# TensorE's order moved one part ahead in a mixture-of-experts step, with two PSUM banks for each kind of result

## The chip, the cores and the metric

The kernel is one program on one core of a Trainium2 chip. The metric is the device time of one execution in microseconds, shown as the median of several executions; one further execution was recorded by the hardware profiler. TensorE is called PE here, VectorE DVE, ScalarE ACT, GpSimd POOL, and SP is the engine that issues most of the DMAs.

## The reference

Four sequences (batches) of 512 tokens and 512 features. Each goes first through a selective state-space block that works on a context input, and then through a mixture of experts. Cut to what matters:

```python
# front: the state-space block, per batch
u = silu(conv(in_proj(ctx)))                     # 512 channels x 512 tokens
delta = softplus(dt_proj(x_proj(u)))             # B, C (16 rows each) from x_proj too
for t in tokens:                                 # 16 states per channel
    state = state * exp(delta_t * A) + (delta_t * u_t) * B_t
    y_t = sum(state * C_t, over the 16 states)
x = x + tanh(g_xattn) * (y + D * u) * silu(layernorm(x))
# feed-forward: the shared expert and 7 routed ones, with top-3 weights w_e
n = layernorm(x)
out = (silu(n @ Ws1) * (n @ Wsg)) @ Ws2
for e in range(7):
    out += w_e * ((silu(n @ W1[e]) * (n @ Wg[e])) @ W2[e])
x = x + tanh(g_ffn) * out
```

All weight matrices of the experts are 512 x 512, and every expert is computed on all tokens.

## The kernel before

The feed-forward work is cut into 32 steps: 4 batches times 8 experts (the shared one is expert 0). Each 512 x 512 x 512 product is made from operands split into a high and a low half, in three passes. In a step, TensorE makes four "up" parts (`up(step, j)`, bank `ps_h1[j % 2]`) and four "gate" parts (`gate(step, j)`, the single bank `ps_hg`), 12 matmuls each, alternately, and then the four outputs (`down_high` and `down_low`, banks `ps_y[i % 3]`), also 12 matmuls each: tiles 0 and 1 together, then tile 2, then tile 3. A step has 144 such matmuls.

Between the parts the other engines make the hidden tile j: ACT's tanh of the up part into `h_tmp[j % 2]` (L857, `t_done`), DVE's first product (L1219, `m_done`), DVE's product with the gate part (L1224, `h_made`), ACT's high half (L863, `hh_ready`), and POOL's low half (L1363, `hl_ready`). DVE adds each output tile to `acc` (`add_out`, L1214, `acc_done`).

The state-space block of the next batch is woven into the steps of the present one, by hand, in slots: `between(0)` to `between(11)` on TensorE and on DVE, two for each hidden tile and four in the outputs. The steps of experts 2 to 6 (five in each of the first three batches; "state steps" below) carry most of it. For each of the 16 states, slots give DVE two multiplications (`bmul`, L1089) and two scans (`scan`, L1098) over 1024 columns each, and four sums (`sum_rows`, L1104); TensorE four groups of four transposes (`state_to_rows`, L538); ACT four decays (`decay`, L791). The first transposes of a state wait for its second scan: on TensorE these stand in the slots 0, 4 and 8 of a state step, and the scan that slot 8 waits for is in DVE's slot 7. ACT runs three decays after each high half, in order; each decay waits for the scan that last read its buffer. In the step of expert 7, DVE finishes the block: `make_y` (L1127), `residual` (L1135, L1138), mean and variance, `make_x2` (L1143), and two of the next convolution's taps (L1000). Then TensorE transposes x2 (L547), ACT and DVE split it (L823, L1151), and the next batch's shared step begins.

In batch 0 the weights are split into halves as they come (ACT: `split_hi`, L848; POOL: L1358, L1369, L1375) and stored; SP loads the stored halves in the later batches (`fetch_part`), each part after TensorE has read its forerunner. SP works through one hand-written queue. The last batch has no state-space work beside it.

Of the kernel before, what the change touches and what calls it, by code (L numbers as in the profile page):

```python
# [28 lines left out]
def gated_block(nc, t, out):  # L29
# [20 lines left out]
    with ExitStack() as ctx:  # L50
# [77 lines left out]
        conv_ps = [ps_h1[0], ps_h1[1], ps_hg, ps_y[0]]  # L128
# [328 lines left out]
        def _(pe):  # L457
# [12 lines left out]
            def in_proj(m, et):  # L470
# [3 lines left out]
                else:  # L474
                    bank = ps_y[1 + et % 2]
# [101 lines left out]
            def up(step, j):  # L577

                weights_ready(0, step, j)
                if j >= 2:  # L580
# [17 lines left out]
            def down_high(step, tiles):  # L598

                for j in range(T):  # L600
                    pe.wait_ge(hh_ready, T * step + j + 1)
                    weights_ready(2, step, j)
                    for i in tiles:
                        three_passes(ps_y[i % 3][:], [h_hi[:, j, i * P:(i + 1) * P]], [half(2, j, 0), half(2, j, 1)],
                                     ((0, 0), (0, 1)), j == 0, False)

            def down_low(step, tiles):

                for i in tiles:
                    for j in range(T):  # L610
                        pe.wait_ge(hl_ready, T * step + j + 1)
                        mm = pe.matmul(ps_y[i % 3][:], h_lo[:, j, i * P:(i + 1) * P], half(2, j, 0),  # L612
                                       start=False, stop=j == T - 1)
                    mm.then_inc(y_done, 1)

            def step_(step, between=lambda g: None, before_down=None):
# [6 lines left out]
                if some(step):  # L623
                    pe.wait_ge(acc_done, T * step)
# [836 lines left out]
```

## Time and profile before

| | |
|---|---|
| median of 3 executions | 1498.68 us (1497.59 to 1501.57) |
| profiled execution, its own time | 1496.58 us |
| profiled execution, span from first to last instruction | 1494.5 us |
| TensorE busy | 1397.6 us (94%) |
| DVE busy | 1053.1 us (70%) |
| ACT busy | 510.0 us (34%) |
| POOL busy | 453.6 us (30%) |
| mean granted TensorE clock | 0.968 |

The busy time of TensorE is modelled from pipelined matmuls, so how far apart matmuls start says more than how long one is shown. The granted clock is a share of 2.4 GHz.

### The profile page before, as it was taken

To read this page: it belongs to the slowest core of one execution; us is meant where nothing else is said; L and a number is where in the kernel's file an instruction comes from. 1 tells how busy PE (TensorE), PEld (TensorE's weight loads), DVE (VectorE), ACT (ScalarE), POOL (GpSimd) and SP (SyncE) were. 2 spreads that over 40 slices of the span, in tenths; PEclk is the share of its full clock that TensorE was granted. 3 is DMA by queue.
4 is the path that set the end of the run, shared out by engine and by line. 5 is a ranking of instruction groups with operands and counts; after the bars stand their busy time and mean duration, and the time that the engine had idled before them with its cause. 6 is when DMAs were issued, how large, how long until landed. Compare 5 with 4: busy or idle time off the path is not lost.

```text
span 1494.5 us, 18163 instructions
## 1 busy us (share of the span) xinstructions
PE 1397.6 (94%) x6311; PEld 1078.6 (72%) x6311; DVE 1053.1 (70%) x1259; ACT 510.0 (34%) x855; POOL 453.6 (30%) x240
## 2 busy tenths in 40 slices
PE   8599869999999989999999979999999999999999
PEld 4244456877777776787787867787778878888887
DVE  5898855899998974588999874689999853222222
ACT  3676625544444323432322223432332211111111
POOL 3200004687777721123323211122332211111111
PEclk9599989999999999999999999999999999999999
DMA  6111634567765574455555564455555554655552
GB/s 206 43 64 57 252 121 171 204 248 272 243 244 206 212 249 141 143 192 179 177 173 181 174 247 128 143 184 179 185 176 172 184 191 156 210 194 191 189 168 84
DMA packets 90796, 266.36 MB, mean 178 GB/s; under 512 B 11472, under 2 KB 11600, under 8 KB 90336
## 3 DMA queue, kind: packets, MB, share of 16 engines
q1 hardware_dynamic: 85472, 258.39, 51.0%
q10 hardware_dynamic: 5248, 6.96, 1.3%
q8 instruction: 47, 0.77, 0.2%
q14 instruction: 29, 0.24, 0.0%
HBM read 207.39 MB, written 57.93 MB: 178 GB/s over the span
## 4 chain that ended last, share of the span: by engine, by line
PE 68%; DVE 18%; issue 6%; ACT 5%; DMA 2%; SPq 1%; POOL 0%; ACTq 0%; DVEq 0%; POOLq 0%
PE ps_hg L461 19%; PE ps_h L461 18%; PE ps_y L461 12%; PE ps_y L612 7%; DVE st L1098 7%; PE ps_mid L538 5%; DVE y_rows L1104 3%; ACT dA L791 2%; PE ps_h L530 2%; DVE st L1089 1%; DVE u L1000 1%; PE ps_mid L508 1%; DVE h_tmp L1224 1%; PE ps_mid L501 1%; DVE h_tmp L1219 1%
## 5 line engine op out<-in xcount | busy, mean ns | idle before, releaser
L1363 POOL TENSOR_TENSOR h_lo<-h_tmp,h_hi 128x512 fp32r<-128x512 f32 x128 | 280.8, 2194 | 781.7 <-ACT h_hi L863 781.7
L461 PE MATMUL ps_h<-x_hi,w_split 128*128 128x512 f32 x1024 | 350.8, 404 | 9.0 <-issue 4.6
L461 PE MATMUL ps_hg<-x_hi,wg_split 128*128 128x512 f32 x1024 | 349.8, 403 | 3.4 <-DVE h_tmp L1224 3.4
L1098 DVE TENSOR_TENSOR_SCAN st<-dA,st 128x1024 f32<-128x1024 f32 x128 | 298.5, 2341 | 0.0
L461 PE MATMUL ps_y<-w_split,h_hi 128*128 128x512 f32 x1024 | 258.2, 400 | 0.8 <-ACT h_hi L863 0.8
L461 PEld LDWEIGHTS ps_h<-x_hi,w_split 128*128 128x128 f32 x1024 | 195.1, 191 | 50.8 <-issue 6.9
L863 ACT ACTIVATE h_hi<-h_tmp 128x512 fp32r<-128x512 f32 x128 | 81.0, 632 | 430.6 <-DVE h_tmp L1224 430.6
L461 PEld LDWEIGHTS ps_hg<-x_hi,wg_split 128*128 128x128 f32 x1024 | 195.3, 191 | 44.4 <-issue 4.2
L461 PEld LDWEIGHTS ps_y<-w_split,h_hi 128*128 128x128 f32 x1024 | 190.3, 190 | 40.0 <-ACT h_hi L863 2.0
L1219 DVE SCALAR_TENSOR_TENSOR h_tmp<-h_tmp,ps_h 128x512 f32<-128x512 f32 x128 | 87.8, 686 | 182.8 <-ACT h_tmp L857 182.4
L461 PE MATMUL ps_hg<-x_lo,wg_split 128*128 128x512 f32 x512 | 202.1, 395 | 0.0
L461 PE MATMUL ps_h<-x_lo,w_split 128*128 128x512 f32 x512 | 201.7, 394 | 0.0
L538 PEld LDWEIGHTS ps_mid<-ident,st 128*128 128x128 f32 x1024 | 124.1, 141 | 94.3 <-issue 49.7
L1089 DVE TENSOR_TENSOR st<-u,b_all 128x1024 f32<-128x1024 f32 x128 | 179.2, 1411 | 10.4 <-PE ps_mid L538 10.3
L538 PE MATMUL ps_mid<-ident,st 128*128 128x128 f32 x1024 | 154.8, 277 | 29.7 <-DVE st L1098 27.1
L791 ACT ACTIVATE dA<-delta,neg_A 128x511 f32<-128x511 f32 x256 | 168.3, 710 | 34.5 <-DVE st L1098 27.9
L857 ACT ACTIVATE h_tmp<-ps_h 128x512 f32<-128x512 f32 x128 | 76.0, 593 | 298.8 <-PE ps_h L461 298.6
L1224 DVE TENSOR_TENSOR h_tmp<-h_tmp,ps_hg 128x512 f32<-128x512 f32 x128 | 87.6, 685 | 101.7 <-PE ps_hg L461 101.4
L1104 DVE SCALAR_TENSOR_TENSOR y_rows<-ps_mid,c_cols,y_rows 128x512 f32<-128x512 f32 x192 | 142.0, 740 | 0.0
L612 PE MATMUL ps_y<-w_split,h_lo 128*128 128x512 f32 x512 | 134.4, 394 | 0.0
L1214 DVE SCALAR_TENSOR_TENSOR acc<-ps_y,coef,acc 128x512 f32<-128x512 f32 x112 | 82.5, 736 | 59.1 <-PE ps_y L612 58.9
L461 PEld LDWEIGHTS ps_h<-x_lo,w_split 128*128 128x128 f32 x512 | 98.3, 192 | 18.5
(140 smaller groups left out, 1133.5 us busy)
## 6 DMA issues: line engine op xcount, KB each, us to landing
w_split<-split_scratch SPq DMA_DIRECT2D x192, 512.0 KB, 4.9
wg_split<-split_scratch SPq DMA_DIRECT2D x96, 512.0 KB, 4.2
split_scratch<-w_split SPq DMA_DIRECT2D x64, 512.0 KB, 4.3
b_all<-xd_scratch SPq DMA_DIRECT2D x64, 256.0 KB, 4.0
split_scratch<-wg_split SPq DMA_DIRECT2D x32, 512.0 KB, 3.1
w_raw<-in_W_dram SPq DMA_DIRECT2D x14, 1024.0 KB, 7.6
wg_raw<-in_Wg_dram SPq DMA_DIRECT2D x7, 1024.0 KB, 10.0
dA<-in_x_dram SPq DMA_DIRECT2D x4, 1024.0 KB, 11.0
```

The source lines that it names most:

```text
L461: mm = pe.matmul(out_, lhs[a], rhs[c], start=first and q == 0, stop=last and q == len(sides) - 1)
L538: mm = pe.transpose(ps_mid[bank][:, et * P:(et + 1) * P], st[n % 2][:, et, i * P:(i + 1) * P], ident[:])
L612: mm = pe.matmul(ps_y[i % 3][:], h_lo[:, j, i * P:(i + 1) * P], half(2, j, 0), start=False, stop=j == T - 1)
L791: act.activation(dA[odd][:, et, 1:L], delta[:, et, 1:L], ACT.Exp, scale=neg_A[:, et, n:n + 1]).then_inc(da_ready, 1)
L863: act.activation(h_hi[:, j, :], h_tmp[j % 2][:], ACT.Copy).then_inc(hh_ready, 1)
L1089: dve.tensor_tensor(st[odd][:, two], u[:, two], b_all[odd][:].rearrange("p (a l) -> p a l", a=1).broadcast_to([P, 2, L]), ALU.mult).then_i ...
L1098: dve.tensor_tensor_scan(flat[1], flat[0], flat[1], 0.0, ALU.mult, ALU.add).then_inc(scan_done, 1)
L1104: dve.scalar_tensor_tensor(out=y_rows[:, i, :], in0=ps_mid[bank][:], scalar=c_cols[:, i, n:n + 1], in1=y_rows[:, i, :], op0=ALU.mult, op1= ...
L1214: dve.scalar_tensor_tensor(out=acc[:, i, :], in0=ps_y[i % 3][:], scalar=scale, in1=before[:, i, :], op0=ALU.mult, op1=ALU.add).then_inc(ac ...
L1219: dve.scalar_tensor_tensor(out=h_tmp[j % 2][:], in0=h_tmp[j % 2][:], scalar=1.0, in1=ps_h1[j % 2][:], op0=ALU.add, op1=ALU.mult).then_inc( ...
L1224: dve.tensor_tensor(h_tmp[j % 2][:], h_tmp[j % 2][:], ps_hg[:], ALU.mult).then_inc(h_made, 1)
L1363: pool.tensor_tensor(h_lo[:, j, :], h_tmp[j % 2][:], h_hi[:, j, :].bitcast(F32), ALU.subtract).then_inc(hl_ready, 1)
```

## The change

TensorE's order in a step becomes: up and gate parts 1 to 3 of this expert, then up and gate part 0 of the *next* expert, then this expert's four outputs, one after the other. The other engines' orders follow: the tanh and the two products of tile 0 of the next step come before this step's `add_out`s; its high half waits for `y_done`, since `h_hi` is single. The slots 0 to 11 keep their numbers, and now lie around parts 1, 2, 3, 0' and the outputs 0 to 3. The last step of each batch (expert 7) has no part ahead; the shared step begins with its own part 0. The eight PSUM banks are divided anew: `ps_hg` gets two, `ps_y` two instead of three. SP's queue is not changed.

```diff
-        ps_hg = ctx.enter_context(nc.psum_tensor("ps_hg", [P, L], F32))
-        ps_y = [ctx.enter_context(nc.psum_tensor(f"ps_y{i}", [P, L], F32)) for i in range(3)]
+        ps_hg = [ctx.enter_context(nc.psum_tensor(f"ps_hg{i}", [P, L], F32)) for i in range(2)]
+        ps_y = [ctx.enter_context(nc.psum_tensor(f"ps_y{i}", [P, L], F32)) for i in range(2)]
@@ tensor
             def gate(step, j):
                 weights_ready(1, step, j)
-                if j >= 1:
-                    pe.wait_ge(h_made, T * step + j)
-                product(ps_hg, 1, j).then_inc(hg_done, 1)
+                if some(T * step + j - 1):
+                    pe.wait_ge(h_made, T * step + j - 1)
+                product(ps_hg[j % 2], 1, j).then_inc(hg_done, 1)
-            def down_high(step, tiles):
-            def down_low(step, tiles):
+            def down(step, i):
+                if some(T * step + i - 1):
+                    pe.wait_ge(acc_done, T * step + i - 1)
+                for j in range(T):
+                    pe.wait_ge(hh_ready, T * step + j + 1)
+                    weights_ready(2, step, j)
+                    three_passes(ps_y[i % 2][:], [h_hi[:, j, i * P:(i + 1) * P]], [half(2, j, 0), half(2, j, 1)],
+                                 ((0, 0), (0, 1)), j == 0, False)
                 for j in range(T):
+                    pe.wait_ge(hl_ready, T * step + j + 1)
+                    mm = pe.matmul(ps_y[i % 2][:], h_lo[:, j, i * P:(i + 1) * P], half(2, j, 0),
+                                   start=False, stop=j == T - 1)
+                mm.then_inc(y_done, 1)
+            def step_(step, ahead=True, between=lambda g: None):
+                for j in range(1, T):
                     up(step, j)
-                    between(2 * j)
+                    between(2 * j - 2)
                     gate(step, j)
-                    between(2 * j + 1)
+                    between(2 * j - 1)
-                down_high(step, (0, 1))
-                between(2 * T)
-                down_low(step, (0, 1))
-                between(2 * T + 1)
-                down_high(step, (2,))
-                down_low(step, (2,))
-                between(2 * T + 2)
-                pe.wait_ge(acc_done, T * step + 1)
-                down_high(step, (3,))
-                down_low(step, (3,))
-                between(2 * T + 3)
+                if ahead:
+                    up(step + 1, 0)
+                between(2 * T - 2)
+                if ahead:
+                    gate(step + 1, 0)
+                between(2 * T - 1)
+                for i in range(T):
+                    down(step, i)
+                    between(2 * T + i)
@@ scalar
+            def h_high(step, j):
+                act.wait_ge(h_made, T * step + j + 1)
+                if j == 0 and some(step):
+                    act.wait_ge(y_done, T * step)
+            def step_(step, ahead=True, between=lambda j: None, after=lambda j: None):
+                for j in range(1, T):
+                    tanh(step, j)
+                    if first_round(step + 1):
+                        split_hi(step + 1, 0, w1h, j)
+                    between(j)
+                    h_high(step, j)
+                    if first_round(step + 1):
+                        split_hi(step + 1, 1, wgh, j)
+                    after(j)
+                if ahead:
+                    tanh(step + 1, 0)
+                between(T)
+                if ahead:
+                    h_high(step + 1, 0)
+                if first_round(step + 1):
+                    split_down(step + 1)
+                if first_round(step + 2):
+                    split_front(step + 2)
@@ vector
+                for j in range(1, T):
+                    hidden(step, j, lambda: between(2 * j - 2))
+                    between(2 * j - 1)
+                if ahead:
+                    hidden(step + 1, 0, lambda: between(2 * T - 2))
+                else:
+                    between(2 * T - 2)
+                between(2 * T - 1)
+                for i in range(T):
+                    between(2 * T + i)
+                    add_out(i)
@@ gpsimd
+                for j in range(1, T):
+                    if first_round(step + 1):
+                        split_up(step + 1, j)
+                    h_low(step, j)
+                    if first_round(step + 1):
+                        split_gate(step + 1, j)
+                    between(j)
+                if ahead:
+                    h_low(step + 1, 0)
+                if first_round(step + 1):
+                    split_down(step + 1)
+                if first_round(step + 2):
+                    split_front(step + 2)
```

`split_front(step)` splits tile 0 of an expert's up and gate weights. In the shared step, the router's columns move from behind gate 0 to behind up 1, and on DVE the convolution's taps stand in tile 0's two products while `front_silu` moves behind tile 1's first product.

## Rows read from the trace of the kernel before

**Rows 1.** The page: busy time by engine, and the chain that ended last.
```profile
PE 1397.6 (94%) x6311; PEld 1078.6 (72%) x6311; DVE 1053.1 (70%) x1259; ACT 510.0 (34%) x855; POOL 453.6 (30%) x240
...
PE 68%; DVE 18%; issue 6%; ACT 5%; DMA 2%; SPq 1%; POOL 0%; ACTq 0%; DVEq 0%; POOLq 0%
```

**Rows 2.** Waits of PE in the whole span: releaser, us in total, times, longest us.
```profile
PE ps_mid L538 <- DVE st L1098: 27.1, 28, 4.2
PE ps_mid L547 <- DVE x_lo L1151: 12.5, 4, 5.1
...
PE ps_hg L461 <- DVE h_tmp L1224: 3.4, 2, 2.8
```

**Rows 3.** Windows: state steps of batches 0 and 1, and a step of batch 3.
```profile
430.00:475.00 45.00, 41.31 (x196) 32.78 (x195) 40.62 (x38) 18.91 (x34) 33.49 (x16) 0.96 0.64 229
690.00:730.00 40.00, 39.09 (x195) 31.48 (x194) 36.24 (x37) 12.27 (x20) 12.80 (x4) 1.00 0.54 177
...
1328.00:1361.00 33.00, 33.00 (x147) 27.35 (x146) 8.77 (x13) 4.92 (x8) 5.15 (x4) 1.00 0.57 191
```

**Rows 4.** Chain in a step of batch 3, one of its up parts: start us, us, what.
```profile
1295.31 2.72 PE ps_h L461 x12
```

**Rows 5.** PE timeline, outputs of a state step in batch 1, with idle before.
```profile
715.79 0.39 PE L461 MATMUL ps_hg<-x_hi,wg_split 128*128 128x512 f32 x1
...
716.62 3.91 PE L461 MATMUL ps_y<-w_split,h_hi 128*128 128x512 f32 x16
720.80 0.66 PE L538 MATMUL ps_mid<-ident,st 128*128 128x128 f32 x4 [0.28 <-DVE st L1098]
...
729.92 0.48 PE L461 MATMUL ps_h<-x_hi,w_split 128*128 128x512 f32 x1
```

**Rows 6.** DVE and ACT timelines, the same stretch.
```profile
716.01 1.21 DVE L1089 TENSOR_TENSOR st<-u,b_all 128x1024 f32<-128x1024 f32 x1
717.14 0.68 DVE L1224 TENSOR_TENSOR h_tmp<-h_tmp,ps_hg 128x512 f32<-128x512 f32 x1
...
718.40 2.28 DVE L1098 TENSOR_TENSOR_SCAN st<-dA,st 128x1024 f32<-128x1024 f32 x1
...
722.77 0.74 DVE L1214 SCALAR_TENSOR_TENSOR acc<-ps_y,coef,acc 128x512 f32<-128x512 f32 x1
...
713.50 0.72 ACT L791 ACTIVATE dA<-delta,neg_A 128x511 f32<-128x511 f32 x1 [1.06 <-DVE st L1098]
714.13 0.58 ACT L857 ACTIVATE h_tmp<-ps_h 128x512 f32<-128x512 f32 x1
```

**Rows 7.** Timelines of a state step in batch 0: PE, then ACT, then DVE.
```profile
448.50 0.66 PE L538 MATMUL ps_mid<-ident,st 128*128 128x128 f32 x4 [2.15 <-DVE st L1098]
...
465.35 0.66 PE L538 MATMUL ps_mid<-ident,st 128*128 128x128 f32 x4 [1.00 <-DVE st L1098]
...
429.72 2.19 ACT L848 ACTIVATE w_split<-w_raw 128x512 fp32r<-128x512 f32 x4 [7.65 <-PE ps_y L612]
432.94 0.60 ACT L857 ACTIVATE h_tmp<-ps_h 128x512 f32<-128x512 f32 x1 [1.02 <-PE ps_h L461]
...
434.83 2.19 DVE L1089 TENSOR_TENSOR st<-u,b_all 128x1024 f32<-128x1024 f32 x1
```

**Rows 8.** Timelines at the end of batch 0: DVE, then PE.
```profile
539.78 0.69 DVE L1219 SCALAR_TENSOR_TENSOR h_tmp<-h_tmp,ps_h 128x512 f32<-128x512 f32 x1 [0.84 <-ACT h_tmp L857]
...
546.43 0.75 DVE L1214 SCALAR_TENSOR_TENSOR acc<-ps_y,coef,acc 128x512 f32<-128x512 f32 x1
...
556.03 0.74 DVE L1214 SCALAR_TENSOR_TENSOR acc<-ps_y,coef,acc 128x512 f32<-128x512 f32 x1
...
558.71 1.94 PE L547 MATMUL ps_mid<-ident,st 128*128 128x128 f32 x8 [5.10 <-DVE x_lo L1151]
```

**Rows 9.** PE timelines of the shared steps of batches 0 and 1.
```profile
222.62 0.47 PE L461 MATMUL ps_hg<-x_hi,wg_split 128*128 128x512 f32 x1 [2.83 <-DVE h_tmp L1224]
...
598.49 5.54 PE L461 MATMUL ps_y<-w_split,h_hi 128*128 128x512 f32 x16
```

More of the change, by code:

```diff
@@ L648, in shared_step @@
                 pe.wait_ge(*taken(b, column_place(b, T - 1)))
-                step_(STEPS * b, between)
+                up(STEPS * b, 0)
+                gate(STEPS * b, 0)
+                step_(STEPS * b, True, between)
             def state_sums(m, first):
@@ L901, in after, with ahead_1, after_1 @@
                         front_ccols(m)
[L902 to L919 removed]
+                tanh(STEPS * b, 0)
+                h_high(STEPS * b, 0)
+                if first_round(STEPS * b + 1):
+                    split_front(STEPS * b + 1)
+                if m is not None:
+                    front_tanh(m)
+                router_columns(b)
+                step_(STEPS * b, True, between, after)
+            def batch(b, m):
+                def ahead_1(j):
+                    if j == T:
+                        decays(m, T, 2 * T)
+                def after_1(j):
+                    if j == 1:
                         router_exp(b)
                         front_z(m, (0, 1))
[L922 removed]
+                    if j == 2:
                         decays(m, 0, 2)
[L924 removed]
+                    if j == 3:
                         front_z(m, (2, 3))
                         decays(m, 2, T)
[L927 to L928 removed]
                 if some(b):
@@ L1203, in router, with hidden, step_ @@
                 assert done[0] == links
-            def step_(step, e, between=lambda p: None):
+            def hidden(step, j, between=None):
+                dve.wait_ge(t_done, T * step + j + 1)
+                dve.scalar_tensor_tensor(out=h_tmp[j % 2][:], in0=h_tmp[j % 2][:], scalar=1.0, in1=ps_h1[j % 2][:],
+                                         op0=ALU.add, op1=ALU.mult).then_inc(m_done, 1)
+                if between:
+                    between()
+                dve.wait_ge(m_done, T * step + j + 1)
+                dve.wait_ge(hg_done, T * step + j + 1)
+                dve.tensor_tensor(h_tmp[j % 2][:], h_tmp[j % 2][:], ps_hg[j % 2][:], ALU.mult).then_inc(h_made, 1)
+            def step_(step, e, ahead=True, between=lambda p: None):
                 def add_out(i):
@@ L1331, in last @@
                         front_conv(m + 1, (1,))
-                step_(STEPS * b, None, shared)
-                step_(STEPS * b + 1, 0, first_routed)
+                hidden(STEPS * b, 0, lambda: front_conv(m, range(DC - 1) if b == 0 else (DC - 2,)))
+                step_(STEPS * b, None, True, shared)
+                step_(STEPS * b + 1, 0, True, first_routed)
                 for e in range(2, NE):
-                    step_(STEPS * b + e, e - 1, lambda p: slot(m, 3 * (e - 2) + 1 + p // T, p % T))
-                step_(STEPS * b + NE, NE - 1, last)
+                    step_(STEPS * b + e, e - 1, True, lambda p: slot(m, 3 * (e - 2) + 1 + p // T, p % T))
+                step_(STEPS * b + NE, NE - 1, False, last)
             for b in range(NB - 1):
@@ L1424, in _ @@
             power(x2var, x2rstd, 0)
-            batch(0, 1)
-            with pool.Fori(1, NB - 1) as b:
+            for b in range(NB - 1):
                 batch(b, b + 1)
-            with pool.Fori(0, STEPS) as e:
+            shared_step(NB - 1)
+            with pool.Fori(1, NE) as e:
                 step_(STEPS * (NB - 1) + e)
+            step_(STEPS * NB - 1, False)
 def kernel(**inputs):
```

165 lines of the change are left out of this document (59 added, 106 removed).

## The prediction

> **What bounds the kernel now.** I read the page first, then PE's waits, then windows by stage, then the chain and the timelines of one step of each kind. The page has PE busy for 94% of the span and on 68% of the chain; DVE has most of the rest [rows 1]. A step of batch 3 is pure TensorE: 33.00 us busy in 33, its clock whole [rows 3], and twelve matmuls take 2.72 us, so one starts every 0.227 us [rows 4]. All 144 need 32.6 us, and nothing waits. So batch 3's seven routed steps have nothing to win, whatever the order. The two waits that the new banks address are small: the gate bank's 3.4 us, in 2 places; waits for scans are 27.1 us, in 28 [rows 2].
>
> In the state steps DVE is nearly as full as PE: 36.24 us of 40 in batch 1, 40.62 of 45 in batch 0 [rows 3]. There the end is set by turns: by PE, and in slots 4 and 8 by the scan that the transposes wait for. At the batch boundaries DVE's chain alone sets it, with PE idle for 5.10 us [rows 8].
>
> **State steps of batches 1 and 2.** The last gate part's last matmul starts at 715.79, the outputs at 716.62. Before slot 8 stand 16 output matmuls, 16 x 0.227 = 3.63 us, so TensorE is free for the transposes at 720.25; it starts them at 720.80 [rows 5]. What comes last is DVE: second product 717.14, sum, scan 718.40 + 2.28 = 720.68 [rows 6]. In the new order only output 0 stands there, 12 matmuls, 2.72 us: TensorE is free 0.91 us earlier. The scan isn't: DVE's slots keep their places around the fourth hidden tile, and that tile's tanh is late because ACT stands at a decay that waits 1.06 us for a scan (713.50, then the tanh at 714.13) [rows 6]; three decays still stand ahead of the tanh. So the wait grows by 0.91 us, and the four matmuls that covered it are done later: 10 steps x 0.9 = +9. The bound below is 0 (the scan comes earlier by as much), above 1.2 each.
>
> The two output banks cost nothing there: output 2 needs `add_out(0)`, which starts at 722.77 and takes 0.74 [rows 6], while TensorE is in output 1 until about 720.80 + 0.4 + 2.9 = 724.1. Output 3 needs `add_out(1)`, after one more sum and scan (0.7 + 2.2), about 727; TensorE comes there 2.9 + 0.4 us after 724.4, about 727.7. It is close.
>
> **State steps of batch 0.** The same 0.9 us. Besides, ACT is released when the outputs are done (429.72), splits four tiles in 2.19 and does the tanh at 432.94, for which it has waited 1.02 us [rows 7]. Now it makes the high half of tile 0 (about 0.6), four splits, 2.19, and two more for the expert after next, 2 x 0.55 = 1.1: 3.9 us instead of 3.2, so the tanh is 0.7 late, and DVE with it. DVE has no slack behind: TensorE stands 2.15 us at 448.50 and 1.00 at 465.35 for its scans [rows 7]. That makes 1.6. POOL's work also comes in one longer run (low half of tile 0, four splits, two more), under DVE's multiplications, of which one takes 2.19 us in batch 0 and 1.21 in batch 1 [rows 6, 7]; one more stretched would add 1.0. I take 2.0, between 1.6 and 2.6: 5 steps, +10 (8 to 13). The Trainium skill (GPSIMD Engine Reference, 1 Specifications) says that GpSimd shares its SBUF interfaces with VectorE and contends with VectorE instructions that have two SBUF inputs, which these have; the rows agree. By that rule the upper end, 13, would be the sum's term; by the rows it may be either.
>
> **Batch boundaries.** TensorE has done up and gate 0 of the last expert ahead, 2 x 2.72 = 5.44 us, inside the step before. The last step is shorter by that, but DVE's chain (sums, make_y, residual, statistics, x2, taps) starts at the same slot as before and so 5.44 us later in TensorE's work. TensorE had idle time there, which it can't use for work already done. DVE gains back one tile's wait, 0.84, and its two products, about 1.2 [rows 8]: 2.1. Net +3.3, at two boundaries. `add_out(0)` at 546.43 stands behind residual and statistics [rows 8]; with two banks output 2 waits for it, about 3 us, and output 3 for the next behind x2. Where the taps follow (they end before the last `add_out`, 556.03) DVE hides this. At the third boundary no taps follow: there I take 4.2, between 3.3 and the whole 5.4. Sum +10.8 (5 to 16). If DVE's chain did not end last, it would be 0.
>
> **What it gains.** In batch 0's shared step gate 1 waits 2.83 us for the single bank, behind the convolution's taps [rows 9]; now nothing waits, but `front_silu` moves back on DVE, behind a tanh that stands behind the router's columns, and `xproj` needs it. I keep 2, between 0 and 2.83 and the slower clock after it. In the shared steps of batches 1 and 2 the first 16 output matmuls take 5.54 us [rows 9] against 3.91 [rows 5], waiting for ACT's high half, for which two parts now stand as cover: 2 x 1.6 = 3.2. Together -5 (-3 to -9). In batch 3's last step the high half of tile 3 is needed 6 matmuls, 1.4 us, after the gate part instead of 12: +0.5. SP's queue is as before: the ahead part's weights wait for `h1_done` counts that now come earlier; I cost it at 0, since the fetch follows the output weights by a few descriptors, issued at the end of the previous step, and TensorE needs it some 16 us later (6 x 2.72). If SP stood at a `load_b` there, the whole delay would show.
>
> **Sum.** 9 + 10 + 10.8 - 5 + 0.5 = +25.3 against the profiled execution, 1496.58 us (span 1494.5 and 2.1 around it): 1521.9. The median is 2.1 above that execution: 1524.0 us.
>
> **Rivals.** Noise is about 0.3%, 4.5 us, from 1498.7.
> - *Forecast, 0.62:* slot 8's wait deeper, batch 0 later, boundaries later: 1524, its own range 1511 to 1534.
> - *The clock falls too, 0.15.* Batch 0's windows show a granted clock of 0.96 where TensorE stood for 2.15 us, batch 1's 1.00 with short waits [rows 3, 5, 7]. The new waits at slot 8 are 1.2 us in batches 1 and 2 and near 2 in batch 0. If they suffice, each step loses 0.04 x 45 = 1.8 us: 10 to 15 steps, +18 to +27, about 1547. Against it: 1.2 us is nearer to the 0.28 to 1.0 us after which nothing is seen than to 2.15. The Trainium skill (TensorE: Matmul & The Clock Gate, Part 1) says that the half rate is the default and activity releases it; it would speak for this case.
> - *Faster, 0.08.* The part ahead gives DVE's scan its time, because the decay that holds the fourth tanh becomes free sooner. It decides if the scan ends 1.4 us sooner relative to the gate part: then the 27.1 us of scan waits go [rows 2], and with the -5 and the boundaries' +10.8 the time is 1498.7 - 27 - 5 + 11 = 1478. For it: ACT has no splits in the fourth tile any more. Against: batch 1 has no splits at all and waits the same way. The Trainium skill (Perfetto Trace Analysis, Optimization Strategy) reads one gap that repeats as a sign of too few buffers, as PSUM; the repeating gap here waits for a scan, not for a bank, which the trace says against it.
> - *Only the boundaries cost, 0.15.* DVE's slots move up by the 0.9 us, and POOL's run hides: 10.8 - 5 + 0.5, 1505; with the boundaries' lower bound 1499. That the order does nothing falls here, half of it within the noise.
>
> **Numbers.** Slower 0.83 (the first two and half of the last), same 0.09, faster 0.08. The range reaches to the last rival's upper half and to the clock's: 1502 to 1543.
>
> **What would show it.** In the new profile: the wait of `ps_mid` L538's transposes for scans grows from 27 to about 45 us; state steps of batches 1 and 2 0.9 us longer than the 40 us that a window holds now, those of batch 0 2 us longer than 45 [rows 3]; PE's idle before x2's transposes moves partly to outputs 2 and 3; batch 3's steps stay at 32.6; the 2.83 and the 5.54 go. I am wrong if slot 8's wait stays at 0.3 us, if the granted clock in batches 1 and 2 falls under 1.00, or if TensorE waits for a DMA ahead of a part 0.

## The result, and the profile after

The changed kernel takes 1523.18 us (median of 4, 1522.20 to 1527.27) against 1498.13 (4 runs, 1495.32 to 1501.57) of the kernel before on the same chip: ratio 1.0171, 95% interval 1.0143 to 1.0200. The profiled execution takes 1523.53, its span 1521.7. The prediction said 1524.0, slower.

The page of the changed kernel (busy time, chain), for [rows 1]:

```profile
PE 1401.4 (92%) x6311; PEld 1077.9 (71%) x6311; DVE 1048.1 (69%) x1259; ACT 507.7 (33%) x855; POOL 418.4 (27%) x240
...
PE 63%; DVE 20%; issue 7%; ACT 6%; DMA 2%; SPq 1%; ACTq 0%; POOL 0%; DVEq 0%
```

The busy times are nearly the same but for POOL's (418.4 for 453.6); PE's share of the chain fell from 68% to 63%. Its waits, for [rows 2] (us in total, times, longest):

```profile
PE ps_mid L538 <- DVE st L1117: 42.9, 31, 4.2
...
PE ps_mid L547 <- DVE x_lo L1170: 11.2, 4, 4.6
...
PE ps_y L609 <- POOL h_lo L1387: 4.7, 3, 1.6
...
PE ps_y L461 <- DVE acc L1243: 3.1, 3, 2.1
```

The gate bank's 3.4 us are gone, and the waits for scans grew from 27.1 to 42.9 (about 45 was forecast). The windows, for [rows 3]: two of batch 0, one of batch 1, one of batch 3. After the stretch and its length stand the busy us (and instructions) of PE, PE's weight loads, DVE, ACT and POOL, then the granted clock, the share of the DMA engines and GB/s.

```profile
352.00:397.00 45.00, 40.24 (x184) 31.96 (x184) 38.43 (x36) 16.76 (x30) 28.37 (x16) 0.92 0.62 226
420.00:465.00 45.00, 40.23 (x197) 32.19 (x196) 39.53 (x37) 18.27 (x32) 28.59 (x17) 1.00 0.62 220
700.00:740.00 40.00, 38.19 (x190) 30.69 (x189) 34.92 (x37) 11.54 (x19) 11.16 (x4) 1.00 0.50 178
1290.00:1323.00 33.00, 33.00 (x148) 27.31 (x147) 13.77 (x38) 5.04 (x9) 5.15 (x4) 1.00 0.54 191
```

PE has 38.19 us of 40 in batch 1, where it had 39.09, at a whole clock. The outputs of such a step, PE, then DVE, then ACT, for [rows 5, 6]:

```profile
734.47 0.39 PE L461 MATMUL ps_hg<-x_hi,wg_split 128*128 128x512 f32 x1
...
735.30 2.10 PE L461 MATMUL ps_y<-w_split,h_hi 128*128 128x512 f32 x8
737.24 1.08 PE L609 MATMUL ps_y<-w_split,h_lo 128*128 128x512 f32 x4
739.49 0.65 PE L538 MATMUL ps_mid<-ident,st 128*128 128x128 f32 x4 [1.17 <-DVE st L1117]
...
735.82 0.68 DVE L1232 TENSOR_TENSOR h_tmp<-h_tmp,ps_hg 128x512 f32<-128x512 f32 x1
...
737.08 2.28 DVE L1117 TENSOR_TENSOR_SCAN st<-dA,st 128x1024 f32<-128x1024 f32 x1
...
732.18 0.72 ACT L787 ACTIVATE dA<-delta,neg_A 128x511 f32<-128x511 f32 x1 [1.06 <-DVE st L1117]
732.81 0.58 ACT L851 ACTIVATE h_tmp<-ps_h 128x512 f32<-128x512 f32 x1
```

Set the last gate matmul to zero in both kernels: the tanh starts at -1.66, the scan at +2.61, in both. ACT's decay waits for a scan for 1.06 us in both. DVE and ACT did not move against TensorE; only four matmuls of cover went, and the wait is 1.17 instead of 0.28.

The whole span by stretches, from the starts of the same matmuls in both traces: from a batch's first matmul to the end of expert 1's outputs, the five state steps, and the last expert with the boundary. 5.44 us are put back where a part ran ahead, so that each column holds the same work.

| us | start | shared + expert 1: batch 0, 1, 2 | state steps | last + boundary | batch 3 |
|---|---|---|---|---|---|
| before | 207.0 | 92.8, 87.8, 87.8 | 217.9, 199.3, 199.4 | 44.4, 47.4, 40.3 | 270.3 |
| changed | 208.2 | 91.3, 87.6, 87.0 | 227.5, 203.8, 203.8 | 47.8, 51.4, 44.1 | 269.4 |
| difference | +1.1 | -1.6, -0.2, -0.8 | +9.6, +4.5, +4.4 | +3.4, +4.0, +3.8 | -0.9 |

The differences add to the 27.2 us by which the spans differ.

### The profile page after: what moved, and what is told of

The parts are those of the page before. It is cut to its first block, busy times and chain, and to the rows that moved or that the text cites. A ratio compares the mean times of both kernels' runs of the same rounds, so it can differ in the third digit from the quotient of the medians.

```text
span 1521.7 us, 18382 instructions
## 1 busy us (share of the span) xinstructions
PE 1401.4 (92%) x6311; PEld 1077.9 (71%) x6311; DVE 1048.1 (69%) x1259; ACT 507.7 (33%) x855; POOL 418.4 (27%) x240
## 4 chain that ended last, share of the span: by engine, by line
PE 63%; DVE 20%; issue 7%; ACT 6%; DMA 2%; SPq 1%; ACTq 0%; POOL 0%; DVEq 0%
PE ps_hg L461 18%; PE ps_h L461 16%; PE ps_y L461 12%; DVE st L1117 8%; PE ps_y L609 6%; PE ps_mid L538 5%; DVE y_rows L1123 3%; ACT dA L787 2%; PE ps_h L530 2%; DVE h_tmp L1232 1%; DVE h_tmp L1226 1%; ACT w_split L844 1%; DVE u L1019 1%; PE ps_mid L508 1%; DVE st L1108 1%
## 5 line engine op out<-in xcount | busy, mean ns | idle before, releaser
L1387 POOL TENSOR_TENSOR h_lo<-h_tmp,h_hi 128x512 fp32r<-128x512 f32 x128 | 252.7, 1974 | 893.2 <-ACT h_hi L858 893.2
L1117 DVE TENSOR_TENSOR_SCAN st<-dA,st 128x1024 f32<-128x1024 f32 x128 | 304.9, 2392 | 0.0
L461 PE MATMUL ps_y<-w_split,h_hi 128*128 128x512 f32 x1024 | 264.1, 399 | 5.0 <-DVE acc L1243 3.1
L1226 DVE SCALAR_TENSOR_TENSOR h_tmp<-h_tmp,ps_h 128x512 f32<-128x512 f32 x128 | 87.6, 684 | 229.3 <-ACT h_tmp L851 228.9
L461 PEld LDWEIGHTS ps_y<-w_split,h_hi 128*128 128x128 f32 x1024 | 187.6, 189 | 45.4 <-DVE acc L1243 5.4
L538 PE MATMUL ps_mid<-ident,st 128*128 128x128 f32 x1024 | 156.5, 279 | 46.5 <-DVE st L1117 42.9
L1108 DVE TENSOR_TENSOR st<-u,b_all 128x1024 f32<-128x1024 f32 x128 | 169.9, 1338 | 10.7 <-PE ps_mid L538 10.5
L609 PE MATMUL ps_y<-w_split,h_lo 128*128 128x512 f32 x512 | 138.8, 392 | 4.7 <-POOL h_lo L1387 4.7
L609 PEld LDWEIGHTS ps_y<-w_split,h_lo 128*128 128x128 f32 x512 | 96.2, 188 | 27.3 <-POOL h_lo L1387 6.4
```

Of the source, the lines that this page charges most:

```text
L461: mm = pe.matmul(out_, lhs[a], rhs[c], start=first and q == 0, stop=last and q == len(sides) - 1)
L538: mm = pe.transpose(ps_mid[bank][:, et * P:(et + 1) * P], st[n % 2][:, et, i * P:(i + 1) * P], ident[:])
L609: mm = pe.matmul(ps_y[i % 2][:], h_lo[:, j, i * P:(i + 1) * P], half(2, j, 0), start=False, stop=j == T - 1)
L1108: dve.tensor_tensor(st[odd][:, two], u[:, two], b_all[odd][:].rearrange("p (a l) -> p a l", a=1).broadcast_to([P, 2, L]), ALU.mult).then_i ...
L1117: dve.tensor_tensor_scan(flat[1], flat[0], flat[1], 0.0, ALU.mult, ALU.add).then_inc(scan_done, 1)
L1226: dve.scalar_tensor_tensor(out=h_tmp[j % 2][:], in0=h_tmp[j % 2][:], scalar=1.0, in1=ps_h1[j % 2][:], op0=ALU.add, op1=ALU.mult).then_inc( ...
```

## The experiments

Each was run with the kernel before beside it on the same chip; ratios are to that, medians are in the text. "State steps" are those of the table. The start phase, in which all kernels do the same work, takes 204.1 to 208.3 us in the profiled executions, without an order by kernel that I can see, so I read the stretches and not the spans.

### What the order costs, in parts

Three kernels fill the square between before and the changed one: the new banks with outputs 0 and 1 in pairs or all one by one, each with and without the part ahead.

**outs_alone.** Before's order of parts, the new banks, outputs one by one:

```diff
+                product(ps_hg[j % 2], 1, j).then_inc(hg_done, 1)
...
-                down_high(step, (0, 1))
-                between(2 * T)
-                down_low(step, (0, 1))
-                between(2 * T + 1)
...
+                for i in range(T):
+                    down(step, i)
+                    between(2 * T + i)
```

> The order of parts before the change, with the changed kernel's banks (two for the gate, two for the outputs) and its outputs one after the other; no part ahead. Theory (slot 8 loses cover because one output, 12 matmuls, stands ahead of it instead of 16): state steps of batches 1 and 2 take 0.9 us more than the 40.0 of the kernel before, batch 0's about 0.9 more, the boundaries stay as before, the 2.8 us wait for the gate bank goes: about +9 +4.5 -3 = +10, 1509 us. Rival (the part ahead itself makes the state steps longer): state steps stay at 40.0, 1495 to 1498 us.

Measured: 1548.42 us, ratio 1.0342 (1.0325 to 1.0359), slower than either theory had it. State steps 226.2, 214.8, 214.8. Its waits, and a step's outputs:

```profile
PE ps_y L609 <- POOL h_lo L1350: 28.2, 18, 1.9
PE ps_mid L538 <- DVE st L1085: 16.4, 16, 4.2
PE ps_y L461 <- ACT h_hi L850: 13.4, 26, 2.2
```

```profile
732.52 0.73 PE L461 MATMUL ps_y<-w_split,h_hi 128*128 128x512 f32 x2 [0.28 <-ACT h_hi L850]
735.78 0.50 PE L609 MATMUL ps_y<-w_split,h_lo 128*128 128x512 f32 x1 [1.83 <-POOL h_lo L1350]
```

Output 0 alone needs the fourth high half after 6 matmuls and the fourth low half after 11; in pairs they are needed after 12 and 19. Both come late, so TensorE stands ahead of slot 8 and the scan is no longer what it waits for. What I had seen as a loss at slot 8 alone is a loss of cover, and the next thing to be late takes it.

**banks.** The same without the outputs' order: before with only the banks dealt anew.

```diff
-        ps_hg = ctx.enter_context(nc.psum_tensor("ps_hg", [P, L], F32))
-        ps_y = [ctx.enter_context(nc.psum_tensor(f"ps_y{i}", [P, L], F32)) for i in range(3)]
+        ps_hg = [ctx.enter_context(nc.psum_tensor(f"ps_hg{i}", [P, L], F32)) for i in range(2)]
+        ps_y = [ctx.enter_context(nc.psum_tensor(f"ps_y{i}", [P, L], F32)) for i in range(2)]
...
+                for i in (2, 3):
+                    pe.wait_ge(acc_done, T * step + i - 1)
```

> Before's order with only the banks dealt anew: two for gate and two for the outputs, so that output 2 shares its bank with output 0 and output 3 with output 1; outputs 0 and 1 are still done in pairs, and no part runs ahead. Theory (banks cost nothing, the order does it): state steps of batches 1 and 2 stay at 40.0 us, those of batch 0 at 42.4 to 44.6, the 3.4 us of waits for the gate bank go, the boundaries lose at most 1 us each by output 2 waiting for add_out(0): 1494 to 1501 us. Rival (the third output bank was worth something in every step): output 2 waits for add_out(0) in the state steps, which then take 41 us or more: 1510 us and up.

Measured: 1504.36 us, ratio 1.0051 (1.0034 to 1.0067), between the theories. A state step of batch 1 takes 40.39 instead of 40.04 us, and a routed step of batch 3 33.01 instead of 32.64. In batch 3 output 2 starts 0.2 us late, behind `add_out(0)`; in batch 1 it is output 3 that starts 0.3 us late, behind `add_out(1)`. The third output bank was worth about 0.35 us a step. The second gate bank bought nothing: its waits go, but in batch 0's shared step TensorE then waits 3.8 us for ACT's `xdbl`, and that stretch of the table is 94.2 us for 92.8.

**pairs.** The changed kernel with before's order of the outputs:

```diff
-                for i in range(T):
-                    down(step, i)
-                    between(2 * T + i)
+                high(step, (0, 1))
+                between(2 * T)
+                low(step, (0, 1))
+                between(2 * T + 1)
+                for i in (2, 3):
+                    pe.wait_ge(acc_done, T * step + i - 1)
+                    high(step, (i,))
+                    low(step, (i,))
+                    between(2 * T + i)
```

> The changed kernel, part ahead and banks as they are, but outputs 0 and 1 in pairs as before: 16 high matmuls of both, slot 8, the 8 low ones, slot 9. Theory of the prediction (the step order costs by the four matmuls that no longer stand between the fourth gate part and slot 8): the wait at slot 8 falls from 1.5 back to 0.6 us, state steps of batches 1 and 2 go from 40.9 to 40.0 us, those of batch 0 lose about as much; boundaries stay as in the changed kernel (about 4 us each above before): 1523 - 14 = 1509 us, between 1506 and 1514. Rival (it is the part ahead that makes DVE late, whatever the outputs' order): steps stay at 40.9 and the time at 1520 to 1525 us.

Measured: 1518.16 us, ratio 1.0145 (1.0129 to 1.0162). The steps of batches 1 and 2 do what the theory says: 40.07 us for 40.96, state steps 199.5 for 203.8, and batch 0's lose 3.6. The waits for scans are back at 29.6:

```profile
PE ps_mid L538 <- DVE st L1132: 29.6, 29, 4.2
...
PE ps_y L461 <- DVE acc L1258: 9.0, 4, 2.3
```

The total misses the expected 1506 to 1514. Pairs with two banks wait for `add_out(0)`: 2.3 us at each of the three boundaries (the fourth place, 2.1 us, is in batch 0 and in the changed kernel too), and a step of batch 3 takes 0.37 us more. Against the changed kernel the state steps lose 12.2 us, but the boundaries (47.2, 52.0 and 45.4 now) put back 1.3, batch 3 2.0 and the shared stretches 3.1.

The square, as ratios to before: pairs 1.0051 without and 1.0145 with the part ahead; one by one 1.0342 without and 1.0171 with it. So neither the part ahead nor the outputs' order has a price of its own. The part ahead costs 0.9% beside pairs and gains 1.7% where the outputs go one by one, whose late halves it covers.

### Where the transposes stand

**late8.** The changed kernel with TensorE's slot 8 behind output 1, beside slot 9. DVE's order is as it was.

```diff
-                for i in range(T):
-                    down(step, i)
-                    between(2 * T + i)
+                down(step, 0)
+                down(step, 1)
+                between(2 * T)
+                between(2 * T + 1)
+                for i in range(2, T):
+                    down(step, i)
+                    between(2 * T + i)
```

> The changed kernel with TensorE's slots 8 and 9 both behind output 1; no other engine's order changes. Theory (the wait at slot 8 is bare idle that another output can cover, 1.3 us in 15 state steps): the wait of the transposes for scans falls by some 18 us, state steps of batches 1 and 2 from 40.95 to 39.7 to 40.0, and the time by 14 to 19 us, to about 1507. Rival (DVE's chain bounds the state step and TensorE's wait only moves to output 2 or 3 or to slot 4): within 4 us of 1523.

Measured: 1513.52 us, ratio 1.0121 (1.0100 to 1.0142). State steps 224.6, 199.4, 199.4: batches 1 and 2 are at before's 199.3, and the 0.9 us a step are shown to be the missing cover ahead of slot 8. The time fell by 9.7 us where 14 to 19 were expected: the state steps give back 11.7, but batch 3 has a slow stretch at its start in this execution (272.0 us for 269.4) that the changed kernel's has not.

**late48.** late8, and in the state steps slot 4 behind gate 3:

```diff
                     up(step, j)
-                    between(2 * j - 2)
+                    if j < T - 1 or not late:
+                        between(2 * j - 2)
                     gate(step, j)
+                    if j == T - 1 and late:
+                        between(2 * j - 2)
                     between(2 * j - 1)
```

> The changed kernel with TensorE's slot 8 behind output 1 together with slot 9 (as in late8) and, in the state steps, slot 4 behind the gate part 3 instead of the up part 3. Theory (the waits for scans at slots 4 and 8 are a matter of where TensorE's order places the transposes, and DVE has the slack): the 0.96 us at slot 4 go as the 1.5 us at slot 8 did: state steps of batches 1 and 2 fall from 40.0 in late8 to 39.3 us, batch 0's by 1 to 2: 1500 to 1507 us. Rival (DVE's chain sets the steps once slot 8 is late): the steps stay at 40.0, the wait moves to slot 5 or to the up part of the step ahead: 1512 to 1516 us.

Measured: 1498.38 us (10 runs), ratio 1.0013 (1.0002 to 1.0025), a little below the theory's range. State steps 222.0, 194.5, 194.5: two moved places give back nearly all that the change lost. **before_late** does the same to the kernel before (slot 4 behind gate 2's products, slot 8 behind the low passes of outputs 0 and 1):

```diff
                     up(step, j)
-                    between(2 * j)
+                    if j != 2 or not late:
+                        between(2 * j)
                     gate(step, j)
+                    if j == 2 and late:
+                        between(2 * j)
...
                 down_high(step, (0, 1))
-                between(2 * T)
                 down_low(step, (0, 1))
+                between(2 * T)
                 between(2 * T + 1)
```

> The kernel before, its banks and its order, with slot 4 behind the gate part and slot 8 behind the low passes of outputs 0 and 1 in the state steps. Theory (the scan waits are placement only): its 27 us of waits for scans fall under 8, the state steps of batches 1 and 2 go from 40.0 to 39.0 us, batch 0's by 1 to 2 each: 1478 to 1488 us. Rival (without a part ahead the order has no more cover: output 0's low pass and the next step's first tile wait instead): 1493 to 1503 us.

Measured: 1485.03 us, ratio 0.9922 (0.9905 to 0.9938), faster than before. Its PE waits:

```profile
PE ps_y L612 <- POOL h_lo L1369: 11.4, 13, 1.4
PE ps_mid L538 <- DVE y_rows L1110: 10.4, 13, 1.5
...
PE ps_mid L538 <- DVE st L1104: 4.2, 1, 4.2
```

Of the 27.1 us for scans [rows 2] 4.2 are left, at one place outside the state steps. State steps 213.2, 196.0, 195.9 (39.35 us a step, 39.0 was expected). With late slots the whole change (part ahead, banks and outputs' order together) is worth 1.5 us in each of batches 1 and 2 (194.5), and costs 8.8 in batch 0 and 3.4, 4.2 and 3.8 at the boundaries.

### Batch 0: the splits

**splitgap.** The changed kernel; ACT and POOL do the tile-0 splits of the expert after next in the fourth tile's gap, ahead of the high half and not in the run behind the outputs:

```diff
+                if first_round(step + 2):
+                    act.wait_ge(h_made, T * (step + 1) + 1)
+                    split_front(step + 2)
                 if ahead:
                     h_high(step + 1, 0)
                 if first_round(step + 1):
                     split_down(step + 1)
-                if first_round(step + 2):
-                    split_front(step + 2)
```

> The changed kernel with tile 0's weights of the expert after next split on ACT and POOL before the high half of tile 0, where both stand idle in the outputs (5 to 9 us on ACT, 15 on POOL), instead of behind the splits of the output weights. Theory (ACT's two more splits make the first tanh of a step late, and POOL's run stretches DVE's multiplications): only batch 0's state steps change, each 1 to 2 us shorter, 1515 to 1518 us. Rival (batch 0's slot 4 waits for DVE's own work, stretched by POOL wherever POOL's splits stand): batch 0 within 2 us in total, about 1522.

Measured: 1517.16 us, ratio 1.0152 (1.0122 to 1.0182). Only batch 0's state steps answer to the edit, 224.9 for 227.5; 4 us of the span lie in the start phase. So 2.6, less than the theory's 5 to 10 and near the rival's 2: slot 4 still waits 2.9 to 3.2 us in four of the five steps. In the second step it waits 2.14, and there the scan that it waits for takes 2.27 us, in the others 3.3 to 3.4.

**late48_split** has this edit on top of late48.

> late48 and splitgap together: slots 4 and 8 late, and ACT and POOL do the two tile-0 weight splits of the expert after next in the fourth tile's gap. Theory (in batch 0 the long run of splits behind the outputs holds the tanh and so DVE): batch 0's state steps fall from 44.5 to 43 us or less, five of them, 1491 to 1494 us. Rival (with the slots late the tanh is no longer what TensorE waits for; POOL's run under DVE's multiplications and scans is): batch 0's state steps stay within 0.5 us of 44.5, 1496 to 1500 us.

Measured: 1488.79 us, ratio 0.9945 (0.9923 to 0.9966), below the theory's range. Batch 0's state steps are 214.8 for 222.0, a step 42.5 to 43.4. The first tanh of a step comes at least 0.5 us earlier in all five steps, but the last step gains nothing by it (43.37 us for 43.23). The first step gains 2.2, its tanh 1.0 us earlier. The three in the middle gain 1.3 to 1.9 us, and in each of them one scan takes 2.28 us that took 3.37. That scan and POOL's work beside it, in late48, then in late48_split:

```profile
371.88 1.28 POOL L1400 TENSOR_TENSOR wg_split<-wg_raw,wg_split 128x512 fp32r<-128x512 f32 x1
371.94 3.37 DVE L1124 TENSOR_TENSOR_SCAN st<-dA,st 128x1024 f32<-128x1024 f32 x1
```

```profile
369.70 2.28 DVE L1125 TENSOR_TENSOR_SCAN st<-dA,st 128x1024 f32<-128x1024 f32 x1
369.86 3.20 POOL L1395 TENSOR_TENSOR h_lo<-h_tmp,h_hi 128x512 fp32r<-128x512 f32 x1 [0.19 <-ACT h_hi L865]
```

So 1.1 us of each middle step goes with where POOL's instructions lie against DVE's scans, and an earlier tanh alone gained nothing in the last one. The edit moves the splits of both engines at once, so no run separates ACT's share from POOL's. One edit alone gave 2.6, since TensorE then stood at slots 4 and 8 all the same.

### The boundaries

**bound.** The changed kernel with the last step's slots two parts earlier, packed two by two:

```diff
                def last(q):
+                    if q < 2:
+                        slot(m, DS, 2 * q)
+                        slot(m, DS, 2 * q + 1)
+                    elif q < 2 * T:
+                        last_(q + 2)
```

> The changed kernel with the last step of each of the first three batches getting its state sums and the end of the block two parts earlier (TensorE's four groups behind up 1 and gate 1, DVE's in the same two slots, everything after them two slots earlier). Theory (the boundary costs 3.4 to 3.9 us each because DVE's chain starts two parts late in TensorE's work): each boundary 3 to 5 us shorter, the waits of output 2 for acc gone, 1509 to 1514 us, about 11 less than the changed kernel. Rival (the boundary is set by the transposes of x2 and ACT's and DVE's split of them, not by when the chain starts): within 3 us of 1523.

Measured: 1529.46 us, ratio 1.0225 (1.0202 to 1.0248), outside both ranges; the boundaries grow to 48.5, 52.5 and 46.7. Packed transposes stop TensorE for 1.7 and 1.2 us, since a pair shares what it waits for on DVE, and `add_out(0)` now stood behind x2:

```profile
555.48 1.92 DVE L1163 TENSOR_SCALAR st<-z,mv,rstd 128x512 f32<-128x512 f32 x4 [1.12 <-POOL rstd L1387]
557.32 1.60 DVE L1244 SCALAR_TENSOR_TENSOR acc<-ps_y,coef,acc 128x512 f32<-128x512 f32 x2
```

This edit brought new waits of its own, so it does not tell the theories apart.

**edge** does: late48 with the last expert's part 0 not run ahead. The last step does four tiles as before, and expert 6's slots 6 and 7 stand behind its output 0.

```diff
-                    step_(STEPS * b + e, True, state_sums(m, 3 * (e - 2)), True)
-                step_(STEPS * b + NE, False, state_sums(m, DS - 1))
+                    step_(STEPS * b + e, e < NE - 1, state_sums(m, 3 * (e - 2)), True)
+                last_step(STEPS * b + NE, state_sums(m, DS - 1))
```

> late48 with the last expert's first up and gate part not run ahead: expert 6's step ends without a part ahead (its slots 6 and 7 stand behind output 0), and the last step of a batch does its four tiles with DVE's slots where they are in the kernel before. Batch 3 keeps its part ahead. Theory of the prediction (the boundaries lose because DVE's closing chain starts one part later in TensorE's work): the last step and boundary fall from late48's 47.8, 51.3 and 44.2 us to about 44.4, 48.2 and 42.1 us, the values of outs_alone, -8 to -9 in all; expert 6's step, without cover for the high and low halves, gets 1.5 to 3 us longer in each of three batches, +4 to +9: 1493 to 1501 us. Rival (the boundaries lose by the outputs' order and the two banks, not by the part ahead): they stay within 1 us of late48's and the time rises to 1502 to 1510 us.

Measured: 1504.97 us, ratio 1.0053 (1.0036 to 1.0070). From the last step's first matmul to the next batch's it takes 43.7, 48.1 and 42.1 us: what the theory says, and 9.2 less than late48's 47.8, 51.3 and 44.2. So the boundaries lose mainly by the part ahead; the outputs' order and banks leave -0.7, +0.7 and +1.8 against before. The time itself lies in the rival's range, because expert 6's step costs more than I had put: +3.4 in batches 1 and 2, +6.7 in batch 0. The place, at the end of batch 1, POOL and then PE:

```profile
840.12 3.17 POOL L1416 TENSOR_TENSOR h_lo<-h_tmp,h_hi 128x512 fp32r<-128x512 f32 x1 [2.96 <-ACT h_hi L878]
...
843.35 0.50 PE L609 MATMUL ps_y<-w_split,h_lo 128*128 128x512 f32 x1 [1.60 <-POOL h_lo L1416]
...
849.76 2.11 PE L461 MATMUL ps_y<-w_split,h_hi 128*128 128x512 f32 x8 [1.07 <-DVE acc L1267]
```

Taking the part away at one place uncovers what it covered there, by one and a half times what it saved.

### A version faster than both

**third_bank.** before_late (the cut is against it, and the next one's against third_bank; both hold for the state steps), whose third output bank lets output 2's high passes run before the low ones of output 0:

```diff
                 down_high(step, (0, 1))
+                down_high(step, (2,))
-                down_low(step, (0, 1))
+                down_low(step, (0,))
                 between(2 * T)
+                down_low(step, (1,))
                 between(2 * T + 1)
-                down_high(step, (2,))
                 down_low(step, (2,))
```

> before_late (before's order and banks, slots 4 and 8 late), and in the state steps the third output bank is used: the high passes of output 2 stand right behind those of outputs 0 and 1, then low 0, slot 8, low 1, slot 9, low 2. Theory (what is left in a state step is one wait of 0.74 us of output 0's low pass for POOL's low half of tile 3, which eight more matmuls cover): 15 steps, those of batches 1 and 2 fall from 39.35 to 38.6 us: 1485 - 11 = 1474 us. Rival (output 3 then waits for add_out(0), which comes eight matmuls later on DVE): steps stay at 39.3, 1483 to 1487 us.

Measured: 1479.42 us, ratio 0.9882 (0.9865 to 0.9898), between the theories. The wait for POOL is gone, but in batches 1 and 2 a step takes 39.24 us for 39.35: the cover was spent at the next late thing, slot 0.

```profile
682.62 0.65 PE L538 MATMUL ps_mid<-ident,st 128*128 128x128 f32 x4 [0.57 <-DVE st L1108]
```

Batch 0, at 206.7 for 213.2, has most of the gain; the boundaries take 3.1 us more in all. **slots_048** moves slot 0 behind gate 0 as well:

```diff
-                    if j != 2 or not late:
+                    if j in (1, 3) or not late:
                         between(2 * j)
                     gate(step, j)
-                    if j == 2 and late:
+                    if j in (0, 2) and late:
                         between(2 * j)
```

> third_bank with slot 0 behind gate part 0 as well, beside slot 1, in the state steps. In third_bank the one wait left over 0.3 us in a state step of batch 1 is 0.72 us at slot 0, whose scan is released late because output 0's sum is later. Theory (placement again: DVE has slack over the step, 36.5 us of 39.2): the wait goes, steps of batches 1 and 2 fall from 39.24 to 38.5 us: 1479 - 10 = 1469 to 1473 us. Rival (DVE's and ACT's chain of decays, scans and hidden tiles now sets the step's length): steps stay at 39.0 to 39.3, the wait shows at slot 4 or 8 instead: 1476 to 1481 us.

Measured: 1472.94 us, ratio 0.9837 (0.9821 to 0.9854). Steps of 38.4 us; state steps 206.6, 191.8, 191.8. A window of batch 1:

```profile
700.00:740.00 40.00, 40.00 (x203) 33.04 (x202) 37.71 (x37) 12.93 (x22) 14.42 (x5) 1.00 0.56 187
```

TensorE is busy for all of it, with before's PSUM banks and no part ahead.

## Why the prediction was right, point by point

The total was right, and the terms for batches 1 and 2 and the boundaries were right by their mechanism. That batch 0 came out close is in part luck, and only half of the gains came, as said below. (The chances as written add up to 0.845 for slower, not 0.83.)

- **State steps of batches 1 and 2, +9:** measured +4.5 and +4.4, by the mechanism named: 1.17 for 0.28 us of idle at slot 8 in four steps of each batch, and 0.58 for none in the fifth. late8 and pairs each take it away, by either road (transposes later, or 16 matmuls ahead of them).
- **State steps of batch 0, +10:** measured +9.6, but made up otherwise. The 0.9 us at slot 8 did not come in four of the five steps, where it waits 1.1 us for 1.0; only in the last does it wait 1.78 for none. ACT's run and the late tanh did come, after and in the order ACT, POOL, DVE, PE:

```profile
350.49 0.63 ACT L858 ACTIVATE h_hi<-h_tmp 128x512 fp32r<-128x512 f32 x1 [8.64 <-PE ps_y L609]
351.03 2.70 ACT L844 ACTIVATE w_split<-w_raw 128x512 fp32r<-128x512 f32 x5
...
353.63 0.62 ACT L844 ACTIVATE wg_split<-wg_raw 128x512 fp32r<-128x512 f32 x1
354.15 0.57 ACT L851 ACTIVATE h_tmp<-ps_h 128x512 f32<-128x512 f32 x1
...
352.78 6.05 POOL L1399 TENSOR_TENSOR w_split<-w_raw,w_split 128x512 fp32r<-128x512 f32 x4
...
354.76 0.69 DVE L1226 SCALAR_TENSOR_TENSOR h_tmp<-h_tmp,ps_h 128x512 f32<-128x512 f32 x1 [2.40 <-ACT h_tmp L851]
...
370.22 1.11 PE L538 MATMUL ps_mid<-ident,st 128*128 128x128 f32 x4 [3.21 <-DVE st L1117]
```

  From release to tanh ACT needs 3.66 us, 0.44 more than before's 3.22 (0.7 was forecast), DVE stands 2.40 for it, and TensorE's wait at slot 4 is 3.21 for 2.15 [rows 7]. But in the four steps behind the first the late tanh is made up for before slot 4: its scan starts 16.3 us after the step's first matmul before the change and 16.2 after it. What grew there is the scan, by 1.08 us, as much as the wait. (In the first of the five the scan was long before the change too, and it starts later.) DVE and then POOL before the change, and POOL and then DVE after it:

```profile
446.17 2.27 DVE L1098 TENSOR_TENSOR_SCAN st<-dA,st 128x1024 f32<-128x1024 f32 x1
446.33 3.19 POOL L1363 TENSOR_TENSOR h_lo<-h_tmp,h_hi 128x512 fp32r<-128x512 f32 x1 [0.19 <-ACT h_hi L863]
```

```profile
366.75 1.26 POOL L1393 TENSOR_TENSOR wg_split<-wg_raw,wg_split 128x512 fp32r<-128x512 f32 x1
366.82 3.35 DVE L1117 TENSOR_TENSOR_SCAN st<-dA,st 128x1024 f32<-128x1024 f32 x1
```

  After the change POOL is in the middle of its run when the scan starts. So the forecast's POOL term (one more stretched instruction of DVE's, 1.0) is the one that came, in four steps; its 0.9 at slot 8 and ACT's 0.7 mostly did not. By the distances between matmul starts, slot 4 has 5.1 of the 9.6, slot 8 2.1 (1.7 of them in the last step), waits for `y_rows` 1.5 and the slower clock about 1.4; small differences take back 0.5.
- **Boundaries, +10.8:** measured +11.2. outs_alone, without the part ahead, has 44.4, 48.2 and 42.1: so the part ahead is all of the 3.4 at the first boundary, 3.2 of the 4.0 at the second and 2.0 of the 3.8 at the third, and edge shows it too. The rest is the outputs' order and the banks, which the forecast did not count there. The detail was less right as well. Outputs 2 and 3 were to wait for sums, output 2 about 3 us; such waits are 0.48 and 0.51 us at the boundaries (the third and longest, 2.09, is in batch 0's step of expert 1), since TensorE comes to them later by 0.57 and 1.57 us of waits in output 0. PE, then DVE, at the end of batch 0:

```profile
559.63 2.14 PE L461 MATMUL ps_y<-w_split,h_hi 128*128 128x512 f32 x8 [0.48 <-DVE acc L1243]
571.15 1.94 PE L547 MATMUL ps_mid<-ident,st 128*128 128x128 f32 x8 [4.59 <-DVE x_lo L1170]
574.69 0.79 PE L461 MATMUL ps_h<-x_hi,w_split 128*128 128x512 f32 x1 [1.60 <-DVE x_lo L1170]
...
558.83 0.75 DVE L1243 SCALAR_TENSOR_TENSOR acc<-ps_y,coef,acc 128x512 f32<-128x512 f32 x1
```

- **Gains, -5:** measured -2.6; here a step failed. In batch 0 1.6 came, 2 was forecast, but not simply as the gate bank's wait: its 3.4 us are gone, and 2.1 for `add_out` and 1.6 for `xdbl` are new. banks has no gate wait either, and its stretch got 1.4 us longer, so the bank alone gives nothing; what the rest of the order gave is not separated. And of the 5.54 us for 16 output matmuls [rows 9] I had said that they wait for ACT's high half. Their granted clock says otherwise; a window of before over them, and two of the changed kernel, at the start of batch 1 and over its first outputs:

```profile
598.49:603.95 5.46, 5.46 (x17) 4.10 (x17) 2.83 (x5) 1.27 (x4) 0.84 (x1) 0.69 0.18 72
```

```profile
574.69:580.00 5.31, 5.31 (x13) 4.15 (x14) 0.00 (x0) 0.00 (x0) 0.00 (x0) 0.50 0.30 116
622.22:627.77 5.55, 5.55 (x27) 4.59 (x26) 2.73 (x5) 5.31 (x8) 0.00 (x0) 1.00 0.01 3
```

  At 0.69 TensorE was at half rate (1.2 GHz) for part of them: starts 0.43 apart, not 0.227, and nothing waits. In the changed kernel that slow stretch is gone, and the one at the batch's start is longer (13 matmuls, the clock 0.50, for 6). The sum is -0.2 and -0.8, not -1.6 each. A busy time that is long without a wait is to be read together with the clock.
- **Last step, +0.5:** +0.6 (36.7 for 36.1). Batch 3's steps stay at 32.64, as said. The -0.9 of batch 3 has -1.5 from a slow stretch at its start that is not there.
- **Rivals.** The clock's is refuted as a loss: the mean clock is 0.969 for 0.968, and batch 1's is 1.00. In batch 0's state steps it is 0.97 for 0.98, which is the 1.4 us above and not 1.8 a step. "Only the boundaries cost" needed DVE's slots to move up by 0.9 us; they stayed at +2.61. The faster one needed the same.

The Trainium skill's rule that GpSimd contends with VectorE (GPSIMD Engine Reference, 1 Specifications) is borne out by sizes here: DVE's product takes 1.22 us in batch 1 and up to 2.19 in batch 0, its scan 2.28 and up to 3.38. It did not bring the upper end, 13, but by the rows above it set the largest part of batch 0's 9.6, the four longer waits at slot 4.

## What to carry to other kernels

Read what stands between an engine and its next wait as cover, and count it in instructions: here four matmuls were 0.9 us a step. Where another engine has slack over a whole step and TensorE still stands at one place, move that place in TensorE's order before anything else: two transposes' places gave more than banks or a part ahead, and the wait that comes next shows where to move again. Work that is pulled ahead is a gain only where something was uncovered; at a stage's end it is taken from the cover of the chain that closes the stage. When a wait has grown, first compare the duration of the instruction that is waited for in both traces: in batch 0 the scan did not start later, it ran longer.

## What the runs showed of the hardware

TensorE stood idle 3.2 us before slot 4 in each state step of batch 0 of the changed kernel. After the first three (324.54, 370.22, 416.95) it ran at half rate, after the last two (462.58, 507.48) it did not, though the gap was the same 3.6 us from start to start. Two windows behind such gaps:

```profile
370.20:376.00 5.80, 5.78 (x16) 4.72 (x17) 3.35 (x3) 0.05 (x1) 5.71 (x4) 0.50 0.57 215
...
462.60:468.00 5.40, 5.40 (x28) 4.53 (x29) 5.23 (x6) 1.19 (x4) 5.40 (x4) 1.00 0.49 185
```

In the kernel before, gaps of 2.54 us from start to start were followed by it three times of four. What decides was not tried. The same 128 x 512 low half takes POOL 1.29 us in batch 3 and 3.2 beside DVE's scans in batch 1, which is one reason why it came late wherever cover was missing.

Which of the two is slowed goes by which starts first. From 295 us on, the changed kernel has 12 scans that start while an instruction of POOL runs: they take 3.11 to 3.39 us. The other 84 take 2.27 to 2.28, though POOL comes to work under 49 of them, and then it is POOL's instruction that is long, up to 3.3 us. In the kernel before 6 scans are of the first kind (2.55 to 3.38 us), 89 of the second.
